# A two-layer attention, expert and scan kernel on one core: queue orders around attention's last batches, routing in one piece, and 39 slot tiles

## The reference: what is computed

```python
# layer 0
s = attention(xn)            # theta = 0.5 + 0.2*sigmoid(qk) + 0.15*tanh(qk) + 0.1*relu(qk); softmax(theta) @ v
f = xn + routed + shared     # top-1 of 8 experts on the normalized rows, and one shared expert
x = x + s * silu(f)
# layer 1
s = mamba(xn)                # product, convolution of 4 taps, silu, softplus step sizes, scan over 512 tokens, 16 states
f = ffn(xn)                  # gated, 384 hidden
x = x + s * silu(f)
```

## Time and profile before

| | us |
|---|---|
| median of 3 runs | 785.29 (785.2 to 786.74) |
| the profiled execution, its own time | 785.32 |
| its span, first to last instruction | 783.5 |
| PE busy | 668.7 (85%) |
| DVE busy | 639.0 (82%) |
| POOL busy | 533.2 (68%) |
| ACT busy | 502.3 (64%) |

### The profile page before, as it was taken

One profiled execution on the slowest core, in us unless ns is written; L12 is line 12 of the kernel. 1 busy time (PEld: TensorE's weight loads), 2 busy tenths in 40 slices (PEclk: granted clock), 3 DMA queues, 4 the chain that ended last, 5 costly groups with the idle time before them and its releaser, 6 DMA issues. The chain is left out here.

```text
span 783.5 us, 12667 instructions
## 1 busy us (share of the span) xinstructions
PE 668.7 (85%) x3984; PEld 497.9 (64%) x3984; DVE 639.0 (82%) x1088; ACT 502.3 (64%) x1022; POOL 533.2 (68%) x338
## 2 busy tenths in 40 slices
PE   1898969999766879679699899998998998997885
PEld 0875545555444445547488777776877777777765
DVE  5878844666575567559889999999999999999998
ACT  1565633444544556738868878879878787797553
POOL 1002762545572211557798899999999999999995
PEclk9999998999997989889899999999999999999999
DMA  7800114221540004003423615615435236055000
GB/s 210 267 1 14 51 52 116 69 69 58 71 52 0 1 1 163 28 27 136 100 64 110 164 39 150 162 41 155 118 109 132 71 120 165 33 158 149 1 10 18
DMA packets 43233, 67.65 MB, mean 86 GB/s; under 512 B 6296, under 2 KB 30368, under 8 KB 43168
## 3 DMA queue, kind: packets, MB, share of 16 engines
q1 hardware_dynamic: 31888, 48.42, 19.4%
q0 software_dynamic: 9552, 17.85, 11.2%
q10 hardware_dynamic: 1728, 0.57, 0.3%
HBM read 46.08 MB, written 9.74 MB: 71 GB/s over the span
## 5 line engine op out<-in xcount | busy, mean ns | idle before, releaser
L1826 DVE TENSOR_TENSOR_SCAN xnT_all<-psum,nfT_all 128x1024 f32<-128x1024 f32 x128 | 288.4, 2274 | 0.0
L1313 PEld LDWEIGHTS psum<-W_out,xnT_all 128*128 128x128 f32 x2048 | 238.4, 194 | 55.9 <-issue 53.2
L1313 PE MATMUL psum<-W_out,xnT_all 128*128 128x128 f32 x2048 | 243.6, 278 | 28.3 <-DVE work L1842 26.1
L1525 ACT ACTIVATE psum<-delta,A 128x511 f32<-128x511 f32 x256 | 165.1, 683 | 64.1 <-DVE xnT_all L1826 63.3
L1293 POOL TENSOR_TENSOR nfT_all<-attn_all,du 128x1024 f32<-128x1024 f32 x64 | 157.5, 2591 | 2.2 <-DVE xnT_all L1826 2.2
L1293 POOL TENSOR_TENSOR nfT_all<-nf_rows,du 128x1024 f32<-128x1024 f32 x63 | 147.5, 2364 | 14.1 <-DVE nfT_all L1973 12.1
L1842 DVE SCALAR_TENSOR_TENSOR work<-psum,Cc,work 128x128 f32<-128x128 f32 x300 | 82.3, 338 | 6.6 <-PE psum L1313 6.6
L806 POOL DMA_INDIRECT xs_dram<-nf_rows,pos x32 | 33.6, 1049 | 67.1 <-DVE pos L996 57.6
L818 POOL DMA_INDIRECT moe_dram<-nf_rows x40 | 38.5, 962 | 48.5 <-ACT nf_rows L942 48.5
L1313 PE MATMUL psum<-vo_all,W_taps 128*128 128x512 f32 (+3 forms) x128 | 58.9, 606 | 2.8 <-DVE attn_all L681 2.8
L1193 POOL TENSOR_TENSOR du<-du,res_all 128x512 f32<-128x512 f32 x8 | 10.1, 1268 | 70.9 <-ACT du L1534 70.9
(11 more groups left out here) (225 smaller groups left out, 1173.3 us busy)
## 6 DMA issues: line engine op xcount, KB each, us to landing
nf_rows<-bt_dram SPq DMA_DIRECT2D x32, 512.0 KB, 4.8
attn_all<-bt_dram SPq DMA_DIRECT2D x32, 512.0 KB, 3.9
delta<-rl POOLq DMA_DIRECT2D x7, 512.0 KB, 7.0
e<-ab POOLq DMA_DIRECT2D x7, 512.0 KB, 5.7
delta<-e POOLq DMA_DIRECT2D x7, 512.0 KB, 6.3
xs_dram<-attn_all SPq DMA_DIRECT2D x4, 645.0 KB, 8.7
nf_rows<-xs_dram SPq DMA_DIRECT2D x40, 64.5 KB, 1.9
x_all<-in_x_dram SPq DMA_DIRECT2D x8, 256.0 KB, 6.3
```

What stands on the lines that cost most here:

```text
L1313: return nc.tensor.matmul(o, l, r, start=start, stop=stop)
L1525: ins = nc.scalar.activation(dA[:, i % RA, k, 1:L], delta[:, p, h, 1:L], ACT.Exp, scale=A[:, h, 2 * q + k:2 * q + k + 1])
L1826: nc.vector.tensor_tensor_scan(hring[:, i % R, :, :].rearrange("p n l -> p (n l)"), dA[:, i % RA, :, :].rearrange("p n l -> p (n l)"), dbx ...
```

## The change

Four things are changed. The numbers of arithmetic operations stay the same but for one expert tile.

1. `TILES`, the largest number of slot tiles that 4096 tokens in 8 experts can need, is 39 and takes the place of 40 in all loops.
2. On DVE, routing's pieces bases, slots and positions stand together behind theta(0) of batch 0.
3. In batches 3 to 7 the points of `prep` are moved on PE (point 0 behind values(0) and shared_up(1)), a point 1 is added on DVE (between theta(1) and shared(1)) and a point 4 on DVE and PE, and many pieces go to other points. POOL's gathers 4 to 7 go between the first gatings.
4. The convolution of scan batch 1 runs inside batch 7, into PSUM banks 6 and 5, instead of behind it. `gates(7)` stands behind that convolution's outputs on ACT, and the statistics of batches 5 and 6 stand in round 0.

```diff
+    TILES = (NT * P + NE * (P - 1)) // P
...
 # attention round, PE
                 turn(0)
                 scores(b, 2)
+                values(0)
+                shared_up(b, 1)
                 if prep:
                     prep(b, 0)
-                values(0)
-                shared_up(b, 1)
                 turn(1)
                 scores(b, 3)
                 if prep:
                     prep(b, 1)
                 values(1)
+                if prep:
+                    prep(b, 4)
...
 # attention round, DVE
                     routing(1)
+                    routing(2)
+                    routing(3)
...
                 theta(1)
-                if routing:
-                    routing(2)
+                if prep:
+                    prep(b, 1)
                 shared(1)
-                if routing:
-                    routing(3)
...
                     routing(4)
+                if prep:
+                    prep(b, 4)
                 residual()
...
 # POOL
+                for b in range(FIRST + 1):
+                    gathered(b)
                 for i in range(NB - 1):
                     gated(i)
+                    if i + FIRST + 1 < NB:
+                        gathered(i + FIRST + 1)
...
 # PE, first_preparation and rounds
-                        pe.wait_ge(S["res"], at(NB - 1, "res", 1))
+                        pe.wait_ge(F["xT"], 3)
+                        pe.wait_ge(M["xv"], at6(1, "xv", 1))
+                        pe.wait_ge(S["attn"], at(NB - 1, "attn", 1))
...
-                    elif (b, s) == (FIRST + 2, 1):
+                    elif (b, s) == (FIRST + 2, 2):
                         pe.wait_ge(M["xv"], at6(0, "xv", KH))
-                        turn(1)
-                    elif (b, s) == (FIRST + 2, 2):
-                        pe.wait_ge(F["xT"], 2)
...
                     elif (b, s) == (FIRST + 3, 1):
                         pe.wait_ge(M["rl"], at6(0, "rl", 1))
-                        turn(2)
+                        turn(1)
...
+                    elif (b, s) == (FIRST + 4, 4):
+                        pe.wait_ge(S["shh"], at(b, "shh", KI))
+                        x_in(1, 1)
...
+                    elif (b, s) == (FIRST + 4, 3):
+                        x_in(1, 0)
+                        pe.wait_ge(S["res"], at(b, "res", 1))
+                        turn(2)
...
-                pe.wait_ge(S["attn"], at(NB - 1, "attn", 1))
-                pe.wait_ge(S["shh"], at(NB - 1, "shh", KI))
-                x_in(1, 0)
-                x_in(1, 1)
...
 # ACT, first_preparation
-                    if (b, s) == (FIRST, 3):
+                    if (b, s) == (FIRST, 1):
                         gates(0)
                         gates(1)
...
                     elif (b, s) == (FIRST + 2, 0):
-                        roots(1)
                         conv_silu(0, 1)
-                    elif (b, s) == (FIRST + 2, 1):
-                        turned(1)
...
                         nc.scalar.activation(ssmT[0:RX, :], o[0:RX, :], ACT.Copy).then_inc(M["ssm"], 1)
+                        roots(1)
...
-                        turned(2)
+                        turned(1)
...
-                        gates(5)
...
-                        gates(6)
+                        gates(5)
...
+                        gates(6)
...
+                    elif (b, s) == (FIRST + 4, 3):
+                        turned(2)
...
-                act.wait_ge(F["col"], 1)
                 decays(0, 0, 0, True)
-                gates(NB - 1)
                 conv_silu(1, 0)
                 conv_silu(1, 1)
+                gates(NB - 1)
...
 # DVE, first_preparation and round 0
                         clear()
-                    elif (b, s) == (FIRST + 1, 0):
                         statistics(0)
                         moments(0)
-                    elif (b, s) == (FIRST + 1, 2):
+                    elif (b, s) == (FIRST + 1, 1):
                         norms(0)
-                    elif (b, s) == (FIRST + 2, 0):
-                        conv_gate(0)
+                    elif (b, s) == (FIRST + 1, 3):
                         statistics(1)
                         statistics(2)
                         moments(1)
+                    elif (b, s) == (FIRST + 2, 1):
+                        conv_gate(0)
                     elif (b, s) == (FIRST + 2, 2):
                         conv_gate(1)
+                    elif (b, s) == (FIRST + 2, 3):
+                        statistics(3)
+                    elif (b, s) == (FIRST + 3, 0):
                         norms(1)
-                    elif (b, s) == (FIRST + 3, 0):
-                        statistics(3)
                     elif (b, s) == (FIRST + 4, 0):
                         statistics(4)
-                    elif (b, s) == (FIRST + 4, 2):
-                        statistics(5)
                     elif (b, s) == (FIRST + 4, 3):
+                        dve.wait_ge(S["pT_sb"], at(b, "pT_sb", TPB))
+                        first_columns(1)
+                    elif (b, s) == (FIRST + 4, 4):
+                        first_columns(0)
...
+                        if q == 1 and not end:
+                            statistics(NB - 3)
+                            statistics(NB - 2)
```

More of the change, by code:

```diff
@@ L792, in _ @@
                 sp.dma_start(dst, src).then_inc(s_lw, 16)
-            for u in range(SLOT_TILES - XN):
+            for u in range(TILES - XN):
                 sp.wait_ge(E["xT_ps"], u + 1)
@@ L814, in _ @@
             pool.sem_inc(s_o, 16)
-            for u in range(SLOT_TILES):
+            for u in range(TILES):
                 pool.wait_ge(E["y"], u + 1)
@@ L820, in _ @@
             for u in range(UN):
-                pool.wait_ge(s_out[u], 16 * (SLOT_TILES // UN))
+                pool.wait_ge(s_out[u], 16 * ((TILES - u + UN - 1) // UN))
         @block.tensor
@@ L902, in _ @@
             up(0)
-            for u in range(SLOT_TILES):
-                if u + 1 < SLOT_TILES:
+            for u in range(TILES):
+                if u + 1 < TILES:
                     up(u + 1)
-                if u + 2 < SLOT_TILES:
+                if u + 2 < TILES:
                     load_expert(u + 2)
-                if u + 2 < SLOT_TILES:
+                if u + 2 < TILES:
                     turn_x(u + 2)
@@ L912, in _ @@
                 turn_h(u)
-            dn(SLOT_TILES - 1)
+            dn(TILES - 1)
         @block.scalar
@@ L954, in _ @@
                     y_out(u - 1)
-            y_out(SLOT_TILES - 1)
+            y_out(TILES - 1)
         @block.vector
@@ L1118, in xn1 @@
                 return ts[:, i, :, :] if i < LATER else xnb[:, :, :]
-            bM, Gb = (4, 5), (6, 7)
+            bM, Gb, bX2 = (4, 5), (6, 7), (6, 5)
             last_gate = G1[:, (NB - 1) % 2, :].rearrange("p (j d) -> p j d", d=D)
@@ L1178, in _, with gathered @@
             def _(pool):
-                pool.wait_ge(S["res"], at(FIRST - 1, "res", 1))
-                for b in range(NB):
+                def gathered(b):
                     if b >= 2:
@@ L1499, in _ @@
                 queries_keys, scores, shared_up, attend = attention_pe(pe)
-                pe.wait_ge(E["y"], SLOT_TILES)
+                pe.wait_ge(E["y"], TILES)
                 queries_keys(FIRST)
@@ L1523, in decays @@
                         act.wait_ge(M["scan"], at6(b, "scan", i + 1 - RA))
+                        if first:
+                            act.wait_ge(F["col"], h + 1)
                         for k in range(2):
@@ L1560, in conv_silu @@
                 def conv_silu(c, h):
-                    o = bank[bM[h]] if c else bank[7]
+                    o = bank[7] if c == 0 else bank[bX2[h]] if c == 1 else bank[bM[h]]
                     act.wait_ge(M["xv_ps"], at6(c, "xv_ps", h + 1))
@@ L1874, in conv_gate @@
                         w("yh", h + 1)
-                        nc.vector.scalar_tensor_tensor(xv[:, h, :], tc_[:, h, :], 1.0, bank[bM[h]],
+                        nc.vector.scalar_tensor_tensor(xv[:, h, :], tc_[:, h, :], 1.0, bank[(bM if end else bX2)[h]],
                                                        ALU.add, ALU.mult).then_inc(M["xv"], 1)
@@ L1923, in round_, with first_columns @@
                             gate()
+                def first_columns(i):
+                    nc.vector.memset(dA[:, i, :, 0:1], 0.0).then_inc(F["col"], 1)
                 def first_preparation(b, s):
@@ L1965, in first_preparation @@
                             .then_inc(M["delta"], 1)
-                        dve.wait_ge(S["pT_sb"], at(b, "pT_sb", TPB))
-                        nc.vector.memset(dA[:, :, :, 0:1], 0.0).then_inc(F["col"], 1)
                         w("delta", 1)
@@ L1982, in _ @@
                 attended(NB - 1)
-                statistics(NB - 2)
                 rounds(dve, round_)
```

5 lines of the change are left out of this document (3 added, 2 removed).

## The result

The changed kernel takes 773.99 us in the median of 4 runs (773.79 to 779.13), the kernel before 785.25 in 4 runs beside it: a ratio of 0.987, 95% interval 0.9827 to 0.9913. By the medians that is 11.3 us less where 18.4 were forecast; the ratio is one of means, and by it the gain is some 10 us, since one execution took 779.13. The profiled execution took 773.97 us, its span is 772.1.

The account below looks back on a forecast made before the run. Seven scan rounds were taken as bound by full DVE and POOL, the stretch before them by waits between strictly ordered queues. Terms −6.0, −1.9, −9.2, −5.1, −3.3, +5.4, +1.7 sum to −18.4: 766.9 us from 785.3, range 761.5 to 776.

Parts of the forecast that it names:

- rival (a): Attention: most POOL gatings run beside thetas and stretch about eight by 1 us each, giving 775 us; chance 0.20.
- step 3: Batch 4: earlier gates, statistics without their POOL wait and norms sooner bring group 0's transposition forward; −9.2 us.
- Step 1: Batch 0 routing in one piece: earlier scatters, first expert tile no longer waits for its load; −6.0 us, bounds −3.5 and −6.5.
- Step 2: Expert tiles: 39 instead of 40 saves one row-write interval; −1.9 us, bounds −1.5 and −1.9.
- step 5: Batch 7 and the passage: convolution between batch 7's products, second scan starts earlier; −3.3 us, bounds 0 and −5.5.
- Step 4: Batches 5 and 6: group 1's norms leave batch 5, where PE waited for them; −5.1 us, bounds −2 and −7.
- Step 6: After the passage: third scan waits for POOL's last gating, +5.4 us; two statistics move into round 0, +1.7 us.
- (b): Expert start, batches 4 and 7: neither clock nor port costs anything, about 763.2 us; chance 0.13.
- (c): Routing: batch 0's delay passes whole through attention, loads still end last, start gains only 1 us, 772 us; chance 0.06.
- (d): All 32 POOL gating operations of 1.26 us meet DVE operations on its path, giving 807.2 us, slower; chance 0.04.

## Why the prediction was right or wrong

Faster was right, and 773.99 lies in the range of 761.5 to 776; the forecast of 766.9 had 7 us too much gain. That the range held is in part luck: its upper end came from rival (a), which looked for the loss in the wrong place, and step 3 went far outside its own bounds of −7 and −10.5. By its steps:

**Step 1, routing, −6.0: right.** Against theta(0) the first row write moved by 6.1 us. The cover was read rightly, attention's product became what the transposition waits for, and the clock gave back its part (1.98 us for 3.78). Alone it is worth 5.6 us by the medians, and undoing it costs 6.5, or 5.6 if each kernel is set against the kernel before in its own runs.

**Step 2, 39 tiles, −1.9: right**, 1.84 to 2.0 us.

**Step 3, batch 4, −9.2: the step that failed, at −1.3.** Its order of events was right: gates early, POOL done early, statistics without their wait, norms a step earlier. Two terms were mis-sized, both for the same reason. Statistics and moments, "about 2 us", took 5.1 (from 211.76 to the next theta at 216.89), and the norms, "some 2 with the reciprocal" beside POOL (2.5 in its own walk, from 233.65 to 236.2), took 4.1. I looked for the price of the overlap at the 128x512 operations of the earlier trace rows, and let one of the four norms lose 1.0 us. But what counts is how often DVE has to ask while POOL is at work, not how large its operations are: three of the six tiny moments each waited out one of POOL's operations. From the moments the delay went to theta, to ACT's probabilities and to PE, which stood 5.78 us. I had kept the lower clock behind one wait of some 4 us; there were two waits, each over 5 us, and the lower clock behind both. My walk along the queues also had no wait of ACT for PE: ACT stood 2.04 us for PE's late up-projection (L632's tanh, at 227.51) before it came to the root. Against the walk, moved by the 9.8 us of the queries, the moments end 3.3 us late, the second theta adds 0.4, the root 2.6 and the norms 1.6, 7.9 in all. The sign given for this step, a wait of PE under 4 us, failed for group 0 (5.71); for group 1 the wait is gone.

The price could have been read before the change. DVE's timeline of the kernel before, at the same moments and norms:

```profile
230.44 1.16 DVE L1786 TENSOR_SCALAR mean<-mean 128x4 f32<-128x4 f32 x1
...
231.69 1.24 DVE L1788 SCALAR_TENSOR_TENSOR var<-tmp,var 128x4 f32<-128x4 f32 x1
...
243.31 2.06 DVE L1807 TENSOR_SCALAR res_all<-x_all,mean,rs 128x128 f32<-128x128 f32 x4
```

The six moments took 3.0 us there (229.95 to 232.93), already beside gated(1). The change didn't bring the collision about; it left it in place and made it worse: 4.2 us for the moments, and 3.85 for the norms instead of 2.06.

Here the rule that I had weighed at step 5 belonged. The Trainium skill (SBUF — State Buffer, section Who interferes with whom) has DVE and GpSimd hold a shared pair of ports for a whole instruction, and names tensor_scalar among the operations that can take it under conditions, not just those with two inputs in SBUF. The trace agrees: the norms have one tensor input, and four took 3.85 us beside gated(2) and 1.12 without it. I used it on five operations and on thetas, not on the small ones that stand next to POOL.

**Step 4, batches 5 and 6, −5.1: right**, at −5.9 from the transposition of group 0 to batch 7's second theta. The norms of group 1 took 3.80 us beside gated(4) ("some 3.5"), where PE's longest wait in that batch is 1.94 us.

**Step 5, the passage, −3.3: right**, at −3.7. The collisions with the five operations cost 2.1 us (1.9 forecast; 3.8 by the rule): two of POOL's operations lay in their way, not three, and each cost about 1 us (a third, which had begun before them, cost 0.15), so the rule holds and only the count was lower.

**Step 6, +5.4 and +1.7: right**: 5.42 and 1.6 us. The gate moved ahead takes the wait away, as that step's reading demands.

**What was not in the sum.** Behind the scan of the first states 2.2 us more are lost to the end: the moments of the last groups (0.5), waits for PE's projections at the end of round 0 (1.1 more than before; the longest is 2.43 us where it was 1.75), and half a microsecond in the last round. The early theta(0) gives 1.7 us back.

**The rivals.** (a), the port, gave 775 and came nearest to the time, and its cause is the right one; its place was not: of 20 second operations of thetas four are stretched, by 2.6 us together, where three were before, by 2.7. (b) falls, clock and port both cost; (c) falls with step 1. (d) stayed far off: only some fifteen DVE operations were stretched at all. Its reading was wrong in part: of theta's four operations only the first reads PSUM. That operation was never stretched; of the other three only the second was.

## What to carry to other kernels

When work moves on one queue, list what the other engines will be doing beside each instruction in its new place, small instructions too. Where two engines exclude each other, count how many operations of the other engine will be waited out, at most one for each instruction, and not busy time: four operations of 0.28 us beside a run of 1.26 us operations took 3.85 us. Look for such operations in the profile before the change too. An engine that is only a third busy can still cost several microseconds by when it runs, and then the remedy is a start that is later, not an operation that is faster. A wait of PE can be worth more than its length, as where the products behind 5.78 and 5.71 us ran at the lower clock.

## What was not expected of the hardware

Operations on 128x4 elements took up to 1.63 us where they take 0.17 alone, ending 0.03 to 0.04 us behind a POOL operation. POOL pays as well: beside the five operations its own take up to 2.14 us instead of 1.26.

The lower clock doesn't follow from the last wait alone. With the two gates moved, PE stood 2.20 us at 219.62 and then ran at the lower level (1.92 us for L569), but stood 2.46 us at 229.16 and ran at the upper one, in the same execution. And the queries of batch 3, behind the same wait of 0.37 us in all, take 1.13 us in some executions and 2.07 in others. Two or three microseconds of what separates single executions may lie there; that was not tried by itself. More lies ahead of theta(0), which starts at times up to 5 us apart in kernels whose beginning is the same; why is open.
